# Two passes of a first block written out and interleaved, and two VectorE passes placed a slot later

## What is computed

```python
# L0_xattn(p = layernorm(x), k_v = ctx)
kv = k_v @ W_k.T + b_k
out = jnp.einsum('bij,bjd->bid', p, kv)
sim = jnp.einsum('bid,bjd->bij', out, kv) * 256 ** (-0.5)
sim = (sim - mu) * jax.lax.rsqrt(var + 1e-6) * ln_gamma + ln_beta
x = x + jnp.tanh(g_xattn[0]) * softmax(sim)

# L0_ffn(flat = layernorm(x)): 64 experts, 4 chosen for each token, 2 shared ones
scores = softmax(flat @ router_w)
_, topk_idx = jax.lax.top_k(flat @ router_w + router_bias, 4)
comb = ...            # the chosen scores over their sum, zero elsewhere
routed = jnp.einsum('ne,nef,efd->nd', comb, silu(flat @ wg) * (flat @ wu), wd)

# L1_ffn(hidden_states = layernorm(x)) is  residual + mlp(rmsnorm(hidden_states))
# and takes both the normalised row and its rms-normalised form
```

## Time and profile before

| | |
|---|---|
| median of 3 runs | 1308.65 us (1303.43 to 1309.83) |
| the profiled execution | 1308.59 us |
| its span, first to last instruction | 1306.8 us |
| mean granted TensorE clock | 0.883 of full speed |
| busy: PE, DVE, ACT, POOL | 81%, 56%, 40%, 25% |
| first block, two passes | 12.3 to 115.4 us |
| first expert product | 119.72 us |
| stream A and the rest | from about 475 us on |

### The profile page before, as it was taken

The page is one execution under the profiler, slowest core; times in us unless marked ns, Lnnn a source line. Parts: engine busy times, 40 slices in busy tenths (PEclk is TensorE's granted clock), DMA queues, the critical chain, the costliest instruction groups (busy, mean ns, idle before and its releaser), DMA issues.

```text
span 1306.8 us, 19055 instructions
## 1 busy us (share of the span) xinstructions
PE 1058.3 (81%) x6622; PEld 672.6 (51%) x6625; DVE 737.2 (56%) x1684; ACT 525.3 (40%) x883; POOL 328.2 (25%) x626
## 2 busy tenths in 40 slices
PE   3235999999999678788798989995263798899997
PEld 2124888888888543332345633744231543475565
DVE  3653444544544546765746511448789576676644
ACT  1111333233333357554554551132474464445534
POOL 5103334433433445422533320001040210000000
PEclk9556999999999778787899999898676798999999
DMA  6001121112130400000000030002000000000000
GB/s 150 11 0 25 37 48 48 38 46 48 42 107 12 137 1 3 2 2 2 2 3 3 4 113 1 1 0 49 1 2 1 2 2 1 1 1 9 9 4 14
DMA packets 62441, 32.06 MB, mean 25 GB/s; under 512 B 47104, under 2 KB 61072, under 8 KB 62112
## 3 DMA queue, kind: packets, MB, share of 16 engines
q1 hardware_dynamic: 62368, 31.10, 9.0%
HBM read 29.64 MB, written 1.05 MB: 23 GB/s over the span
## 4 chain that ended last, share of the span: by engine, by line
PE 69%; DVE 20%; ACT 4%; issue 4%; POOL 2%; SPq 0%; DMA 0%; POOLq 0%; DVEq 0%; ACTq 0%; PEldq 0%
PE bank L745 16%; PE bank L761 8%; PE bank L853 4%; PE bank L1139 3%; DVE mx L2189 3%; PE bank L968 2%; PE bank L1320 2%; PE bank L936 2%; PE bank L1337 2%; PE bank L898 2%; PE bank L1322 2%; PE bank L1071 2%; PE bank L1119 2%; PE bank L1172 1%; DVE mxc L2189 1%
## 5 line engine op out<-in xcount | busy, mean ns | idle before, releaser
L2189 DVE TENSOR_REDUCE mx<-bank 128x2 f32<-128x512 f32 (+1 forms) x176 | 117.8, 689 | 85.9 <-PE bank L1071 44.8
L1660 ACT ACTIVATE prob<-bank 128x512 f32<-128x512 f32 x176 | 102.9, 597 | 105.7 <-PE bank L1119 77.7
L1499 ACT ACTIVATE hhi<-hh 128x512 fp32r<-128x512 f32 x72 | 45.5, 632 | 153.6 <-DVE hh L2026 140.9
L2022 DVE TENSOR_TENSOR hu<-bank,sg 128x512 f32<-128x512 f32 x64 | 44.2, 691 | 102.2 <-PE bank L745 102.2
L745 PE MATMUL bank<-xh,wh 128*128 128x512 f32 x288 | 91.7, 400 | 0.7 <-POOL wl L2618 0.7
L745 PE MATMUL bank<-xlo,wh 128*128 128x512 f32 x288 | 90.6, 396 | 0.0
L745 PE MATMUL bank<-xh,wl 128*128 128x512 f32 x288 | 90.5, 395 | 0.0
L2014 DVE TENSOR_TENSOR hlo<-hh,hhi 128x512 fp32r<-128x512 f32 x72 | 57.1, 793 | 50.7 <-ACT hhi L1499 50.7
L2618 POOL TENSOR_TENSOR wl<-wraw,wh 128x512 fp32r<-128x512 f32 x72 | 80.4, 1117 | 13.0 <-POOL wh L2615 13.0
L1538 ACT ACTIVATE sg<-bank 128x512 f32<-128x512 f32 x72 | 43.1, 598 | 64.9 <-PE bank L745 64.8
L745 PEld LDWEIGHTS bank<-xh,wh 128*128 128x128 f32 x288 | 54.5, 190 | 14.4 <-POOL wl L2618 1.6
(11 more groups left out here) (456 smaller groups left out, 2288.0 us busy)
## 6 DMA issues: line engine op xcount, KB each, us to landing
wraw<-in_L_ffn_wg_dram SPq DMA_DIRECT2D x64, 64.0 KB, 2.2
wraw<-in_L_ffn_wu_dram SPq DMA_DIRECT2D x64, 64.0 KB, 2.3
wraw<-in_L_ffn_wd_dram SPq DMA_DIRECT2D x32, 128.0 KB, 2.4
l_raw<-in_L_ffn_w_dram SPq DMA_DIRECT2D x2, 1024.0 KB, 7.0
mun<-in_L_ffn_mu_dram SPq DMA_DIRECT2D x1, 2048.0 KB, 7.8
xs<-in_x_dram SPq DMA_DIRECT2D x1, 1024.0 KB, 5.9
w1s<-in_L_ffn_W_dram SPq DMA_DIRECT2D x2, 512.0 KB, 7.9
stage<-in_L_ffn_W_in_base_dram SPq DMA_DIRECT2D x1, 1024.0 KB, 7.8
```

Of the source, the lines that this page charges most:

```text
L1499: return act.activation(dst, src, ACT.Copy, scale=scale)
L1660: act.activation(t.prob[k][:, :], bank[3 + n % 2][:, :], ACT.Exp).then_inc(S("probs"), 1)
L2022: tt(hu[k % 2][:, :], bank[4 + (n + 1) % 4][:, :], sg[k % 2][:, :], ALU.mult).then_inc(once("up_used"), 1)
L2189: V.reduce_max(out_, bank[n % 3][:, :].rearrange("p (h t) -> p h t", h=heads), AX, negate=True)\
```

## The change

**The first block** is written out instead of looped. Each half has buffers of its own (a list `first` of two sets), placed behind the experts' buffers, so that they share no memory with `wh` and `wl`. The steps of the two halves stand interleaved, in an order of its own on each engine, and use different PSUM banks. The barriers behind each pass are gone; one clearing of semaphores is left, by POOL behind its last split of expert weights, and the other engines wait for it only behind the experts. POOL splits the weights of the first two pairs ahead of the tokens of the block. PE's first `up` waits for the split tokens of half 0 only; the wait for half 1's and for the low combine weights comes behind it.

**Stream A.** `between(b, 6)` and `between(b, 7)` stand in slot e + 3, at steps 2 and 4, instead of slot e + 2, steps 4 and 5.

```diff
-            with pe.Fori(0, B // 2) as b:
-                ...
-                end_of_batch(pe)
-                pe.wait_ge(once("batch_cleared"), b + 1)
...
+            contexts(0)
+            contexts(1)
+            turn_tokens(0, 1, (6, 7))
+            attend(0)
+            turn_tokens(1, 2, (0, 1))
+            attend(1)
+            turn_tokens(0, 3, (0, 1), True)
+            route(0)
+            turn_tokens(1, 4, (2, 3), True)
+            route(1)
+            turn_combine(0)
+            turn_combine(1)
...
-                if not (isinstance(u, int) and u == 0):
+                if isinstance(u, int) and u == 0:
+                    pe.wait_ge(S("x_split"), 1)
+                else:
                     pe.wait_ge(once("gate_used"), u)
...
             up(0, 0, 0, 0)
+            pe.wait_ge(S("x_split"), HALVES)
+            pe.wait_ge(S("comb_low"), HALVES)
+            end_of_batch(pe)
...
+            for h, t in enumerate(first):
+                copy(t.c[:, :, :], ctxs[:, T0 * h:T0 * h + T0, :]).then_inc(S("c_ready"), 1)
+            for h, t in enumerate(first):
+                act.wait_ge(S("p0"), h + 1)
+                copy(t.cT[:, :], bank[h][0:CD, :]).then_inc(S("cT"), 1)
...
+            tokens_turned(0, 1, (6, 7))
+            attended(0)
+            tokens_turned(1, 2, (0, 1))
+            attended(1)
+            exps0(0)
+            exps0(1)
+            tokens_turned(0, 3, (0, 1))
+            route_exps(0)
+            tokens_turned(1, 4, (2, 3))
+            route_exps(1)
+            combine_high(0)
+            combine_high(1)
...
+            norm0(0)
+            keys0(0)
+            norm0(1)
+            keys0(1)
+            scores0(0)
+            scores0(1)
+            add_attended0(0)
+            norm0(0)
+            add_attended0(1)
+            norm0(1)
+            chosen(0)
+            chosen(1)
+            combine_low(0)
+            combine_low(1)
...
-                                if sl == e + 2 and k < 6:
+                                if sl == e + 2 and k < 4:
                                     between(b, k + 2)
+                                if sl == e + 3 and k in (2, 4):
+                                    between(b, 5 + k // 2)
...
-            with pool.Fori(0, B // 2) as b:
-                ...
-                end_loop(b * 3 + 3)
...
+            step = Steps(pool, S("pool_step_b"))
+            for k in range(SLOTN):
+                if k == 2:
+                    split_tokens(0)
+                    split_tokens(1)
+                split(0, k)
+            with pool.Fori(1, E // 2 // SLOTN) as t:
                 for k in range(SLOTN):
                     split(t, k)
             for k in range(SLOTN):
                 split(E // 2 // SLOTN, k, shared=True)
+            end_loop(3, [n for n in STAGES[2] if n])
```

More of the change, by code:

```diff
@@ L679, in keep_clock, with contexts @@
                     mm(bank[k][:, :], identb[:, :], mask_q[:, :, :], start=True, stop=True, skip_group_check=True)
-            def transposes0(first_bank, strided=False):
+            def contexts(h):
+                t = first[h]
+                pe.wait_ge(S("c_ready"), h + 1)
+                for i in range(T0):
+                    last = pe.transpose(bank[h][0:CD, i * P:(i + 1) * P], t.c[:, i, :], ident[:, :])
+                last.then_inc(S("p0"), 1)
+                pe.wait_ge(S("cT"), h + 1)
+                mm(bank[2 + h][0:CD, :], wkT[:, :], t.cT[:, :], start=True, stop=True).then_inc(S("kvT_ps"), 1)
+                for i in range(T0):
+                    last = mm(bank[4 + h][:, i * CD:(i + 1) * CD], t.cT[:, i * P:(i + 1) * P], wkT[:, :], start=True, stop=True)
+                last.then_inc(S("kv_ps"), 1)
@@ new lines, in _, with stats0 @@
+            step = Steps(dve, S("dve_step"))
+            def stats0(t, src, eps, between=()):
+                step(*[V.bn_stats(t.bn[:, i, :], src(i)) for i in range(T0)])
+                step(*[V.bn_aggr(t.mv[:, i, :], t.bn[:, i, :]) for i in range(T0)])
+                step(ts(t.ve[:, :], t.mv[:, :, 1], 1.0, eps, ALU.mult, ALU.add),
+                     *[stt(out=t.tmp[:, i, :], in0=src(i), scalar=t.mv[:, i, 0:1], in1=w, op0=ALU.subtract, op1=ALU.mult)
+                       for w in between for i in range(T0)])
+                rsqrt(step, t.rs[:, :], t.ve[:, :])
@@ new lines, in norm0, with keys0 @@
+            def norm0(h):
+                t, rows = first[h], xs[:, T0 * h:T0 * h + T0, :]
+                stats0(t, lambda i: rows[:, i, :], 1e-5)
+                step(*[ts(t.xn[:, i, :], rows[:, i, :], t.mv[:, i, 0:1], t.rs[:, i:i + 1], ALU.subtract, ALU.mult)
+                       for i in range(T0)])
+                dve.sem_inc(S("xn"), 1)
+            def keys0(h):
+                dve.wait_ge(S("kv_ps"), h + 1)
+                tt(first[h].kv[:, :, :], bank[4 + h][:, 0:T0 * CD].rearrange("p (i d) -> p i d", i=T0),
+                   bk_row[:, :].unsqueeze(1).broadcast_to([P, T0, CD]), ALU.add).then_inc(S("kv"), 1)
@@ new lines, in scores0 @@
+            def scores0(h):
+                t = first[h]
+                dve.wait_ge(S("sim_ps"), T0 * (h + 1))
+                stats0(t, lambda i: bank[(6, 4)[h] + i // 2][:, i % 2 * N:(i % 2 + 1) * N], 1e-6,
+                       between=[rowsD["L0_xattn_ln_gamma"][:, :]])
+                step(*[stt(out=t.tmp[:, i, :], in0=t.tmp[:, i, :], scalar=t.rs[:, i:i + 1],
+                           in1=rowsD["L0_xattn_ln_beta"][:, :], op0=ALU.mult, op1=ALU.add) for i in range(T0)])
+                step(V.tensor_reduce(t.least[:, :], t.tmp[:, :, :], AX, ALU.max, negate=True))
+                dve.sem_inc(S("l0_ln_done"), 1)
@@ L2598, in _, with split_tokens @@
             pool.sem_inc(once("up_made"), 4)
+            def split_tokens(h):
+                pool.wait_ge(S("xT"), 2 * (3 + h))
+                high = xh[:, :, T0 * P * h:T0 * P * (h + 1)]
+                step(G.tensor_copy(high, first[h].xT[:, :, :]))
+                step(G.tensor_tensor(xlo[:, :, T0 * P * h:T0 * P * (h + 1)], first[h].xT[:, :, :], high.bitcast(F32), ALU.subtract))
+                pool.sem_inc(S("x_split"), 1)
             def split(t, k, shared=False):
```

226 lines of the change are left out of this document (100 added, 126 removed).

## The result

The changed kernel takes **1259.97 us** (median of 4 runs, 1259.57 to 1262.69) against 1308.62 (1303.43 to 1309.83) for the kernel before beside it: ratio 0.964, 95% interval 0.962 to 0.967.

A forecast was written before the change was run, and what follows sets the result against it. In the first block the chain through all engines, not one engine, was the bound; in attention, places where PE waits. 1308.6 - 32.4 (interleaving) - 5.4 (passes a slot later) = 1270.8 us, range 1262 to 1281.

The forecast's parts named there:

- Part one: First block, two passes interleaved: experts start 32.4 us earlier, between 27.5 and 36.5, after holds by POOL.
- The hold on half 1's second normalise: First block: POOL's token split of half 0 delays DVE's small steps by 2.2 us, within 0 to 3.4.
- That on choosing half 0: First block: POOL's token split of half 1 falls on choosing; 0.6 us taken, half 0's loss absorbed in 2.1 us of waiting.
- the undisturbed one: First block's chain without POOL's holds: first expert product at 83.2, 36.5 us earlier than before.
- the 4.1 us of holds: First block: POOL's weight and token splits delay DVE by 4.1 us in sum, within 0 to 9.
- The rival of holds throughout: POOL and DVE collide throughout: holds reach 9 us, the slot change gives little, 1280.4 us; chance 0.08.
- a step of over 1 us beside `xlo`: First block, a sign of the forecast: POOL holds a small DVE step beside xlo for over 1 us.
- the last key copy earlier: Stream A, a sign: in slots after a batch the last key copy comes 1 to 2 us earlier against the slot's start.
- the term of part two: Stream A, two DVE passes a slot later: 5.6 us, less 0.2 in next slots, gives 5.4 us.
- 1.4 us x 4: Stream A: taken gain per slot after a batch, four times, 5.6 us in all; bounds 0 and 10.4.
- The rival that the clock would keep its upper level: Attention stage: shorter PE stretches keep the clock up, four slots give up to 2 us each, 1260.7 us; chance 0.06.

The follow-up runs named there:

- the first profile: Profile of the changed kernel's first run, set beside the kernel before; that run measured 1259.97 us, ratio 0.964.
- the second profile of the changed kernel: Profile of the changed kernel run once more with the program the same word for word; 1261.13 us, ratio 0.965 to the kernel before.

## Why the prediction was right and where it failed

- **Part one** was forecast at 32.4 us by the first expert product (87.3), and the profile has 87.31. The sum fits better than its terms: the scores of half 0 came at 35.30 and not 33.1, since POOL's splits held `xn` to 26.14 (a hold of 2.5 to 2.8 us where I took 1.3, inside the bounds of 0 to 4.2); DVE itself was free 3.5 us later than forecast, of which 1.3 went into its wait for these scores, 2.5 us instead of 3.8. The hold on half 1's second normalise was 2.0 us (I took 2.2). That on choosing half 0 was 1.36 us on the last pair of products and 0.8 on the one before, mostly taken out of the wait for the second router product, as forecast. The chain was 4.3 us behind the undisturbed one at the end of half 1's second normalise (70.81 against 66.5) and 4.9 at the end of PE's turn (86.17 against 81.3); the zero products then took 1.1 us up to the first expert product where I took 1.9, and so the sum met the 4.1 us of holds that I had put in. The rival of holds throughout, 9 us, is out.
- Part of that agreement is luck. The same program started the experts at 90.96 in another profile, with PE's attention products at half speed: the 9.1 us that I took from transposes to readable scores were 9.0 for half 0 in the first profile (26.26 to 35.30) and 10.85 in the second (26.27 to 37.12). The block of before, unchanged in the three kernels where only stream A differs, gave 119.74, 121.76 and 121.79. As timed runs, the block alone was worth 29.4 us (26 to 33 by its interval) in one comparison and 34.5 (29 to 41) in the other. Both values lie in my bounds of 27.5 to 36.5, their intervals reach beyond them.
- **What it said of the rest** held: interleaving and not barriers (28.7 of 32.4), an expert stage as long as before, no wait for exponentials, a step of over 1 us beside `xlo`, the last key copy earlier (2.6 us, where I wrote 1 to 2).
- **The step that failed is the term of part two**, "since the product before the next maximum comes at about 540.6, 0.9 of xno's 1.65 and all of xs's 0.90 count: 1.8", and with it 1.4 us x 4. The row had it otherwise: the maximum behind `xno` needs an older product. PE's products at 540.34 are read by a later maximum. In the changed kernel that maximum starts at once, and with the sum alone moved the slot was 12.5 us, not 11.7. The time of the passes is 2.6 + 2.6 + 1.9 + 1.6 = 8.7 us at the upper level, not 5.6. With the clock down, the one pair of slots at nearly the same clock says the same: behind batch 0, 16.50 us at 0.65 before and 13.89 at 0.63 with the passes moved, 2.6 us.
- **And the clock was put among the rivals with the wrong price**, "up to 2 us each", and its chance at 0.06. The four slots are 7 to 8 us longer with the clock down in three or four of them than with it up, moved or not (53.6 or 53.3 against 46.4; 62.9 or 61.9 against 55.0). The clock fell in all four of them before; of the two profiles of the changed kernel it fell in none of them in one and in three in the other. So of the 16.5 us in the first profile 8.7 are DVE's and 7.8 are the clock's, and of the latter the seven profiles with the passes moved get 2.5 on average. As timed runs, part two was 12 to 13.5 us where I had 5.4: 7 or 8 of the 10.8 us that the forecast missed.
- **The rest of the 10.8 us** lies in the level of the kernel before and in the clock elsewhere. I forecast against 1308.6; in later sets of runs its median was 1308.4, 1302.6 and 1304.5. In the set that holds all three kernels beside each other (1304.49, 1274.64, 1261.13) part one was 29.9 us and part two 13.5, 43.4 in all against my 37.8. The stages behind stream A, in which nothing changed, took 544.9 us before, and 547.5 and 541.9 in the two profiles of the changed kernel; I can't divide it further.
- The rival that the clock would keep its upper level and bring 1260.7 named the time almost exactly, but got there by holds near nothing, which is not what happened.
- What decides in which slot the clock falls stays open. It differs between two profiles of the same program. Both kernels that kept the old start and had PE's waits filled had the clock up in the four slots (0.94 or 1.00), where the three profiles with the passes in place and nothing filled had it down in all four, so by these profiles PE's waits are part of the cause; but filling the changed kernel did not hold it.

## What to carry to other kernels

Before a pass is given a discount for a wait that it hides, follow the wait's own semaphore: which product, by number, does the next instruction need, and when was it done? Where PE idles in a stage whose granted clock falls now and then, a shorter wait can be worth more than its length: here, in four slots, 8.7 us of DVE time, and in clock 7.8 us between the two profiles that were compared first, but only 2.5 us on average over all that were taken. And a single profile of a kernel whose clock moves has a spread of its own (3.6 us at the start of the experts, 7 us in four slots), so such a forecast needs a wider range than the sum of its terms.

## What the runs showed of the hardware

- The granted clock in the rows is not always the speed of the products. In the second profile of the changed kernel it is 1.00 all the way from 12 to 87 us, and eight transposes (L695) take 1.98 us there and sixteen router products (L720) 3.68. In the first profile the same rows take the same time, with 0.50 in the same window. L711 takes 3.78 us in the second profile and 1.99 in the first, both at 1.00. In stream A the clock and the products agree: there the product for one group by key (L1119) takes 0.39 us at 1.00 and 0.60 at 0.50. Second profile, then first:

```profile
64.66 1.98 PE L695 MATMUL bank<-ident,xn 128*128 128x128 f32 x8 [16.84 <-DVEq L2015]
67.33 3.68 PE L720 MATMUL bank<-rw,xT 128*128 128x64 f32 x16 [0.69 <-ACT xT L1520]
60.00:87.00 27.00, 12.43 (x52) 10.85 (x52) 24.57 (x97) 4.76 (x13) 6.86 (x4) 1.00 0.00 1
```

```profile
60.98 1.98 PE L695 MATMUL bank<-ident,xn 128*128 128x128 f32 x8 [19.34 <-DVEq L2015]
63.65 3.68 PE L720 MATMUL bank<-rw,xT 128*128 128x64 f32 x16 [0.69 <-ACT xT L1520]
60.00:87.00 27.00, 14.13 (x58) 12.15 (x60) 23.02 (x81) 5.36 (x14) 6.89 (x4) 0.50 0.00 1
```

The Trainium skill, page "TensorE: Matmul & The Clock Gate", section "Seeing it yourself", warns that the clock events of a trace have been found unreliable on trn2; these rows agree.

- A VectorE pass with one large operand from SBUF and two per-row operands is stretched by POOL too: four passes for `xn` 1.38 us alone and 2.59 beside POOL's splits; two for `xno` 1.65 us beside POOL's product of 128x512 and 0.73 where the changed kernel has them. There POOL runs too, a subtraction and a cast of 128x128, without stretching them: which POOL instructions hold such a pass is not shown.
- DVE's time and the clock's add up in the one slot where both can be read: behind batch 0 moving the passes is worth 2.6 us with the clock up (13.43 to 10.83) and 2.6 with it down (16.50 to 13.89).
